# Attention, output projection and two-layer feed-forward on one core: three weight sums move from the head pairs to the output projection, and the last pair's products are interleaved anew

## The reference

```python
# 1: cross attention, 16 heads of 64; causal, so only the first 512 context rows count
qp = q @ Wq.T
k, v = jnp.split(latent_kv @ Wkv_expand.T, 2, axis=-1)
scores = jnp.where(causal, einsum(qh, kh) / 8, min)
out = softmax(scores) @ vh
x = x + out @ Wout.T
# 2: gated feed-forward whose weights are rounded to -1, 0, 1
scale = 1.0 / jnp.clip(jnp.mean(jnp.abs(w)), 1e-5, None)      # one number per weight matrix
wq = jnp.clip(jnp.round(w * scale), -1, 1) / scale
# rows are normalised and rounded to 8 bits; gate and up: 1024 x 2816 each; down: 2816 x 1024
# 3: a routed mixture of eight experts and a shared one
```

## Time and profile before

| | |
|---|---|
| median of 3 runs | 628.83 us (627.27 to 629.43) |
| profiled execution, its own time | 628.41 us |
| its span | 626.6 us |
| busy, share of the span | PE 97%, DVE 81%, ACT 68%, POOL 31% |
| first head pair's maxima to last pair's, 34.5 to 145.8 us | 111 us |
| output projection with the last pair's products, 145.8 to 200.2 us | 54 us |

### The profile page before, as it was taken

How to read it: one execution, slowest core, us unless ns; L and a number is a source line. 1 busy time by engine, 2 the same in 40 slices (tenths; PEclk the granted TensorE clock), 3 DMA queues, 4 the chain that set the end, 5 groups by cost and what they waited for, 6 DMA issues and landing times.

```text
span 626.6 us, 10596 instructions
## 1 busy us (share of the span) xinstructions
PE 609.7 (97%) x3611; PEld 477.3 (76%) x3625; DVE 507.1 (81%) x882; ACT 427.7 (68%) x563; POOL 193.3 (31%) x174
## 2 busy tenths in 40 slices
PE   7999999998999999999999999999999999999996
PEld 6778888887887444444567888898998989889775
DVE  5888888888787787889899479788696887968787
ACT  4998888889755988888585366649375583846630
POOL 2254445435000233435940310041340403304051
PEclk9999999999999999999999999999999999999999
DMA  8978776865246997936999758696775958769357
GB/s 332 411 304 305 304 306 243 310 268 201 101 141 242 416 366 278 386 129 249 405 357 422 318 199 331 243 355 243 301 301 212 390 216 312 290 235 373 115 176 269
DMA packets 31070, 177.91 MB, mean 284 GB/s; under 512 B 4064, under 2 KB 4064, under 8 KB 14784
## 3 DMA queue, kind: packets, MB, share of 16 engines
q1 hardware_dynamic: 25536, 158.64, 65.9%
q0 software_dynamic: 5504, 18.88, 8.3%
HBM read 154.30 MB, written 23.20 MB: 283 GB/s over the span
## 4 chain that ended last, share of the span: by engine, by line
PE 71%; ACT 13%; DVE 7%; issue 3%; DMA 3%; POOL 2%; DVEq 0%; POOLq 0%; SPq 0%; ACTq 0%
PE BK L2191 11%; PE BK L307 9%; PE BK L1892 8%; PE BK L1935 6%; PE BK L2194 4%; ACT RA L1384 4%; ACT PR L1411 4%; PE BK L313 3%; PE BK L314 3%; PE BK L319 3%; PE BK L2161 3%; PE BK L2149 2%; PE BK L1837 2%; DVE WL L1038 2%; PE BK L2147 2%
## 5 line engine op out<-in xcount | busy, mean ns | idle before, releaser
L2191 PE MATMUL BK<-EX,WH 128*128 128x320 f32 x384 | 99.4, 342 | 0.0
L705 POOL TENSOR_TENSOR WL<-RC,WH 128x2048 fp32r<-128x2048 f32 x7 | 45.5, 6506 | 167.7 <-ACT WH L1592 167.7
L1038 DVE TENSOR_TENSOR WL<-RA,WH 128x2048 fp32r<-128x2048 f32 x40 | 89.3, 2287 | 9.2 <-ACT WH L1592 8.8
L2194 PE MATMUL BK<-EX,WL 128*128 128x160 f32 x336 | 79.2, 236 | 0.0
L1592 ACT ACTIVATE WH<-RA 128x2048 fp32r<-128x2048 f32 x40 | 73.7, 1907 | 0.8 <-PE BK L1935 0.7
L2191 PEld LDWEIGHTS BK<-EX,WH 128*128 128x128 f32 x384 | 69.2, 189 | 0.0
L2194 PEld LDWEIGHTS BK<-EX,WL 128*128 128x128 f32 x336 | 64.1, 191 | 0.0
L655 POOL TENSOR_TENSOR HB<-HB,ND (+2 forms) x26 | 28.7, 1120 | 100.5 <-DVE BH L922 99.9
L1483 ACT ACTIVATE RA<-RA,RT 128x2048 int16<-128x2048 f32 x22 | 43.8, 1999 | 4.1 <-DMA RA<-wbit 2.1
L1701 ACT ACTIVATE HX<-SR 128x320 fp32r<-128x320 f32 x16 | 7.6, 472 | 57.0 <-DVE SR L1088 57.0
L1892 PE MATMUL BK<-TG,XQ 128*128 128x512 bf16 x189 | 42.1, 379 | 0.2
(11 more groups left out here) (335 smaller groups left out, 1666.2 us busy)
## 6 DMA issues: line engine op xcount, KB each, us to landing
RA<-wbit SPq DMA_DIRECT2D x54, 1024.0 KB, 6.8
RA<-wmoe SPq DMA_DIRECT2D x40, 1024.0 KB, 6.6
RC<-wmoe SPq DMA_DIRECT2D x20, 1024.0 KB, 7.9
rows<-ZERO POOLq DMA_DIRECT2D x40, 256.0 KB, 8.3
XG<-rows SPq DMA_DIRECT2D x10, 512.0 KB, 3.6
rows<-YS SPq DMA_DIRECT2D x9, 512.0 KB, 4.1
RA<-wqk SPq DMA_DIRECT2D x7, 640.0 KB, 8.6
RA<-wo SPq DMA_DIRECT2D x4, 1024.0 KB, 7.3
```

Of the source, the lines that this page charges most:

```text
L705: e.tensor_tensor(WL[2][:, at], RC[5][:, :], WH[2][:, at].bitcast(f32), ALU.subtract).then_inc(free_c[5], 1)
L1038: e.tensor_tensor(WL[m][:, q * RAW:q * RAW + RAW], RC[j][:, :], WH[m][:, q * RAW:q * RAW + RAW].bitcast(f32), ALU.subtract)\
L2191: mm = e.matmul(bank[GBK[f]][:, 0:2 * R], WH[m][:, at], EX[:, k, :, :].rearrange("p a b -> p (a b)"), start=k == 0, stop=k == KD - 1)
L2194: e.matmul(bank[GBK[f]][:, 0:R], WL[m][:, at], EX[:, k, 0, :], start=False, stop=False)
```

## The change

Three sums leave the head pairs: chunks 31 and 32 in pairs 3 and 4 (ACT, RA[4]) and chunk 30 in pair 7 (ACT, RA[1]). They are done by ACT after the last pair instead: chunk 30 and chunk 32 through a new buffer `RP`, which lies where the probabilities PR were, chunk 31 through RA[0]. `RP` is one buffer: SP loads chunk 32 into it when ACT has summed chunk 30. `WO_ORDER` becomes 3, 0, 1, 2: ACT writes the high part of block 3 where the sum of chunk 30 stood in pair 7, no longer between the exponentials and `probs_hi`. POOL makes the remainder of block 3 ahead of that of block 1. On PE, k = 6 of tile 0 comes ahead of the last pair's transposes, the matmuls of k = 2, 3 are split by which part of Wout they need, and the transposes are split by head. DVE adds the sums up inside `gate_rows(0)`, and PE's small matmul moves from behind tile 0 into tile 1.

```diff
-WO_IN = (6, 8, 9, 8)
+WO_IN = (4, 8, 9, 8)
-WO_ORDER = (0, 1, 3, 2)
+WO_ORDER = (3, 0, 1, 2)
+        RP = nc.alloc_sbuf_tensor_at("RP", [P, RAW], f32, offset=PR[0].manual_sbuf_range[0])
@@ SP
-            for c in (2, 3, 4):
-                pair_loads(c)
-                sum_load(4, (11, 31, 32)[c - 2], c)
-            with e.Fori(5, NPAIR - 1) as c:
+            pair_loads(2)
+            sum_load(4, 11, 2)
+            with e.Fori(3, NPAIR - 1) as c:
...
+            sum_load(2, 1, None)
+            e.wait_ge(s("wo_p"), 2)
             sum_load(3, 2, None)
-            e.wait_ge(s("wo_p"), 2)
-            sum_load(2, 1, None)
+            e.wait_ge(s("t_pe"), 2 * NPAIR)
+            e.dma_start(RP[:, :], wbit[30]).then_inc(in_x[0], 16)
+            e.wait_ge(s("wo_d"), 2)
+            sum_load(0, 31, None)
             e.wait_ge(s("ot_lo"), NPAIR + 1)
             e.dma_start(NG[:, :], n_gate.partition_broadcast(P)).then_inc(s("norm_in"), 16)
+            e.wait_ge(sum_x[0], 2)
+            e.dma_start(RP[:, :], wbit[32]).then_inc(in_x[0], 16)
@@ POOL
+            e.wait_ge(s("q_pe"), NPAIR)
+            wo_lo(3)
             wo_lo(1)
             e.wait_ge(s("pn"), 4 * NPAIR)
             v_lo(NPAIR - 1)
-            wo_lo(3)
@@ DVE
+            def weight_totals():
+
+                for j in range(2):
+                    e.wait_ge(sum_x[j], (3, 1)[j])
...
+                if t == 0:
+                    weight_totals()
                 o(e.tensor_reduce(col(6)[:, one], zt[:, :], AX.X, ALU.max, apply_absolute_value=True))
+                if t == 0:
+                    weight_scales()
@@ ACT
-                    absum(1, slice(30, 31), 16 * NPAIR)
+                    wo_hi(3)
                 q_split(c)
...
             exponentials(NPAIR - 1)
-            wo_hi(3)
             probs_hi(NPAIR - 1)
             e.wait_ge(s("vp_lo"), NPAIR)
             wo_hi(2)
-            absum_kept(4, 3, 16 * 7, None)
-            absum_kept(3, 2, 16 * (NPAIR + 1), (free_a[4], 6))
             out_hi(NPAIR - 1)
-            absum_kept(2, 1, 16 * (NPAIR + 1), (free_a[3], NPAIR))
+            absum_kept(4, 3, 16 * 5, None)
+            absum_kept(2, 1, 16 * (NPAIR + 1), (free_a[4], 4))
+            absum_kept(3, 2, 16 * (NPAIR + 1), (free_a[2], NPAIR))
+
+            def absum_late(chunk, n):
+                e.wait_ge(in_x[0], 16 * n)
+                e.activation(RP[:, :], RP[:, :], ACT.Abs, accum_out=ACCW[:, chunk:chunk + 1]).then_inc(sum_x[0], 1)
+            absum_late(30, 2)
+            absum(0, slice(31, 32), 16 * (WO_IN[2] + 1))
+            absum_late(32, 3)
@@ PE
+            def wout_part(ks, low):
+                for k in ks:
+                    for O, W in (((OTH, WOL),) if low else ((OTH, WOH), (OTL, WOH))):
+                        e.matmul(bank[YB[0][0]], O[:, k, 0:P], W[k // 2][:, k % 2, 0:512], start=False, stop=False)
             wout(0, 0, (0, 1), True, False)
             e.wait_ge(s("wo_p"), 1)
-            wout(0, 0, (2, 3), False, False)
-            transposes(NPAIR - 1)
+            e.wait_ge(s("ot_lo"), NPAIR)
+            wout(0, 0, (6,), False, False)
+            e.wait_ge(s("wo_hi"), WO_ORDER.index(1) + 1)
+            wout_part((2, 3), False)
+            transposes(NPAIR - 1, (0,))
+            e.wait_ge(s("wo_p"), 2)
+            wout_part((2, 3), True)
+            transposes(NPAIR - 1, (1,))
             attend(NPAIR - 1, False)
-            wout(0, 1, range(4), True, False)
+            wout(0, 1, (0, 1, 2, 3, 6), True, False)
...
-            e.wait_ge(s("wsum"), 1)
-            e.matmul(bank[7][:, 0:2], ONEF[:, :], WS[:, :], start=True, stop=True).then_inc(s("wsum_pe"), 1)
             for t in range(1, NT):
                 wout(t, 0, range(KD), True, True)
                 if t == 3:
                     e.wait_ge(s("wscale"), 1)
-                wout(t, 1, range(KD), True, True).then_inc(s("y_tile"), 1)
+                if t == 1:
+                    wout(t, 1, range(2), True, False)
+                    e.wait_ge(s("wsum"), 1)
+                    e.matmul(bank[7][:, 0:2], ONEF[:, :], WS[:, :], start=True, stop=True).then_inc(s("wsum_pe"), 1)
+                    wout(t, 1, range(2, KD), False, True).then_inc(s("y_tile"), 1)
+                else:
+                    wout(t, 1, range(KD), True, True).then_inc(s("y_tile"), 1)
                 rows_t(t - 1)
```

More of the change, by code:

```diff
@@ L450, in pair_loads @@
                     sum_load(j, c * 3 + 8 + j, c)
-            for c in (2, 3, 4):
-                pair_loads(c)
-                sum_load(4, (11, 31, 32)[c - 2], c)
-            with e.Fori(5, NPAIR - 1) as c:
+            pair_loads(2)
+            sum_load(4, 11, 2)
+            with e.Fori(3, NPAIR - 1) as c:
                 pair_loads(c)
             qk_load(NPAIR - 1)
-            e.wait_ge(free_a[4], 5)
+            e.wait_ge(free_a[4], 3)
             wo_load(0)
-            sum_load(1, 30, NPAIR - 1)
+            e.wait_ge(free_a[2], NPAIR - 1)
+            wo_load(3)
             e.wait_ge(free_a[3], NPAIR - 1)
             wo_load(1)
-            e.wait_ge(free_a[2], NPAIR - 1)
-            wo_load(3)
             e.wait_ge(free_a[0], NPAIR + 1)
             wo_load(2)
-            sum_load(1, 0, NPAIR)
+            sum_load(1, 0, NPAIR - 1)
             e.wait_ge(s("wo_d"), 1)
@@ L844, in _ @@
             out_lo(NPAIR - 1)
-            absum(1, slice(0, 1), 16 * (NPAIR + 1))
+            absum(1, slice(0, 1), 16 * NPAIR)
+            def weight_totals():
+                for j in range(2):
+                    e.wait_ge(sum_x[j], (3, 1)[j])
+                for j, n in ((0, NPAIR + 2), (1, NPAIR), (2, NPAIR), (3, NPAIR), (4, 4)):
+                    e.wait_ge(free_a[j], n)
+                e.tensor_reduce(WS[:, 0:1], ACCW[:, 0:2 * GC], AX.X, ALU.add)
+                e.tensor_reduce(WS[:, 1:2], ACCW[:, 2 * GC:NABS], AX.X, ALU.add).then_inc(s("wsum"), 1)
             def weight_scales():
@@ L881, in gate_scale @@
                     .then_inc(s("gscale"), 1)
[L882 to L886, removed]
-            e.tensor_reduce(WS[:, 1:2], ACCW[:, 2 * GC:NABS], AX.X, ALU.add).then_inc(s("wsum"), 1)
-            e.wait_ge(s("norm_in"), 32)
-            weight_scales()
             gate_rows(0)
@@ L1451, in pair @@
                     if isinstance(c, int):
-                        absum(4, slice(*((10, 11), (11, 12), (31, 32), (32, 33))[c - 1]), c * 16 + 16)
+                        absum(4, slice(9 + c, 10 + c), c * 16 + 16)
                     absum(3, bass.ds(c * 3 + 11, 1), c * 16 + 16)
@@ L1458, in pair @@
                 values_hi(c)
-            for c in (1, 2, 3, 4):
+            for c in (1, 2):
                 pair(c, True)
-            with e.Fori(5, NPAIR - 1) as c:
+            with e.Fori(3, NPAIR - 1) as c:
                 pair(c, True)
@@ L1487, in rounded_down @@
                 raw = down_raw(i)
-                arrived, n = {0: (in_x[0], 2), 1: (s("raw_d"), 1), 2: (in_x[1], 3), 3: (s("raw_e"), 1),
+                arrived, n = {0: (in_x[0], 4), 1: (s("raw_d"), 1), 2: (in_x[1], 3), 3: (s("raw_e"), 1),
                               4: (in_b[0], 6), 5: (in_b[1], 6), 6: (in_b[2], 5), 7: (in_b[3], 5),
@@ L1498, in down_sign @@
                     .then_inc(s("tern_a"), 1)
+            root(e, col(2)[:, 0:1], col(3)[:, 0:1])
             e.wait_ge(s("wscale"), 1)
@@ L1505, in sign @@
                     .then_inc(s("tern_a"), 1)
-            rounded(0, 0)
-            root(e, col(2)[:, 0:1], col(3)[:, 0:1])
-            for j in range(1, 4):
+            for j in range(4):
                 rounded(j, 0)
@@ L1811, in scores, with transposes @@
                         m.then_inc(s("s_pe"), 1)
-            def transposes(c):
-                for h in range(2):
+            def transposes(c, heads=(0, 1)):
+                for h in heads:
                     for n, (i, off) in enumerate(HBLK):
```

5 lines of the change are left out of this document (2 added, 3 removed).

## The result

The change takes 631.60 us in the median of 7 runs (630.04 to 632.30), the kernel before 628.66 us on the same chip (7 runs, 627.27 to 629.43). The ratio is 1.0040, 95% interval 1.0030 to 1.0049: slower, by 2.9 us in the medians. That is clear of the noise, though small. Profiled executions, which the sum of the prediction was made against: 630.04 us after (span 628.3), 628.41 before (span 626.6), +1.6 us.

The account below looks back on a forecast made before the run. PE, busy 97% of the span, was taken to bound the kernel. Terms -0.8 + 2.0 - 0.7 + 2.0 + 0.1 = +2.6 us gave 631.0 from the profiled execution, 631.4 from the median; stated 631.2 us, range 628.6 to 633.3.

Parts of the forecast that it names:

- Two sums out of pairs 3 and 4, -0.8: Head pairs 3 to 6: without ACT's fourth sum they take 62.33 us in place of 63.15, -0.8 us.
- The port block, 2.15 of the range 0 to 2.4: Last pair: DVE's block 0 subtraction waits for all of POOL's block 3 remainder, ending 2.15 us later.
- `attend` +2.0: Last pair: `attend`, released by the late `v_lo`, starts at 155.86 in place of 153.85, +2.0 us.
- k = 6 in the wait, -0.7: Ahead of `attend`: three k = 6 matmuls, formerly behind it, run in PE's wait, -0.7 us.
- The stall, 2.0: Middle of tile 1: PE's small matmul waits for chunk 32's load and sum, 2.0 us.
- E: The end of `attend`, from which the prediction counts the late sums, so that the earlier shift drops out.
- The rest, 0.1: Behind the stall: PE's transposes may wait for DVE's rounding of tile 0, 0.1 us at most.
- The one on the other side, no block: At 142.8: GpSimd does not block VectorE, the stall stays; +0.9 us, 629.6, chance 0.16.
- the one without a stall: Tile 1: sums finish before E + 14.35, so the small matmul doesn't wait; +0.5 us, 629.2, chance 0.12.
- Neither: Last pair and tile 1: no blocking and no stall; -1.2 us, 627.4, chance 0.07.

Follow-up runs that it names:

- Putting them back: Changed kernel with chunks 31 and 32 summed in pairs 3 and 4 again, only chunk 30 late: 630.14 us, ratio 1.0028 to the kernel before.
- memset: Changed kernel with GpSimd filling block 3's remainder with zeros in place of the subtraction: 628.28 us, ratio 0.9996 to the kernel before.
- VectorE first: Changed kernel with chunk 32 in its own buffer and GpSimd starting block 3's remainder only after VectorE's of block 0: 632.52 us, ratio 1.0056.
- second buffer: Changed kernel with chunk 32 loaded into a buffer of its own once the last `attend` is done: 628.84 us, ratio 1.0008 to the kernel before.
- block 1 first: Changed kernel with chunk 32's own buffer, GpSimd's order block 1, `v_lo`, block 3, and new PE, load and sum orders: 627.40 us, ratio 0.9983.
- the first kernel with the sums alone: Kernel before with the three sums moved, one buffer RP, its own product and remainder order, kept chunk 1 loaded late: 638.19 us, ratio 1.0156.
- the second chip: The unaltered change measured once more on another chip against the kernel before: 631.74 us, ratio 1.0045.
- the kernel with chunk 32 later still: Changed kernel with SP loading chunk 32 only after ACT has summed chunk 31: 634.18 us, ratio 1.0091 to the kernel before.
- the experiment with both edits: Changed kernel with block 3's remainder left out as zeros and chunk 32 in its own buffer: 626.64 us, ratio 0.9971 to the kernel before.

## Why the prediction was right

It said 631.2 us, slower, with a range of 628.6 to 633.3; it took 631.60. By its steps:

- **Two sums out of pairs 3 and 4, -0.8.** Measured 0.82 at pair 6. Putting them back cost 1.05 at the last maxima, so the size is 0.8 to 1.05.
- **The port block, 2.15 of the range 0 to 2.4.** DVE's subtraction ended at 146.57, and POOL's, begun at 139.80, would end at 144.43 by its own 4.63 us: 2.14 us apart, as in the one row of before that the number came from. DVE wanted to start a tenth of a microsecond earlier than I had reckoned, so the instruction was longer by 2.30, and the maxima were late by 2.11. The experiment with the memset took the block away and gave back 2.30 at `attend`. The rule of the Trainium skill that the prediction quoted ("SBUF — State Buffer", section "Who interferes with whom": the later of the two blocks fully) agrees with the 4.59 us here: by it DVE would end at 144.43 + 2.29 = 146.72, 0.15 us later than it did. The 6.03 us of the division in the kernel with VectorE first are not a case of that rule as quoted, since the division reads one large tile in SBUF and not two.
- **`attend` +2.0.** 154.90 for 153.85, and 0.82 from the pairs on top: 1.87. `v_lo` was its releaser, as said.
- **k = 6 in the wait, -0.7.** PE reached the small matmul at 173.40, that is 14.39 us after the end of `attend` (159.01); the prediction had 14.35, with these matmuls taken out.
- **The stall, 2.0.** It was 1.41. The mechanism is right and one term too large. The sum of chunk 30 was over at E + 8.49 (predicted 8.5), the load took 4.87 (4.9), and the last sum started at E + 13.40 (13.4). But from there to PE's matmul it took 2.40 us, not 2.96: the row that I took it from the earlier trace rows ends when PE got there, and PE was still busy with its matmuls. It was an upper bound and not a duration. With 2.40 in its place the same sum gives 1.45.
- **The rest, 0.1.** 0.33 us: `attend` 0.07 longer, and the small matmul 0.26 dearer behind a stall. I had not priced the latter.

The steps give -0.82 + 1.87 - 0.69 + 1.41 + 0.33 = +2.1 us, and the end is at +2.13; the prediction's steps had +2.6. Of the +2.13, 0.5 us are made good later, I have not traced where; the profiled execution is +1.6.

**What stays open.** The medians differ by 2.9 and 3.3 us on two chips, the two profiled executions of the change lie 1.6 us above that of before. That the median of 631.6 lies so near to the 631.2 is thus partly luck: the sum was 0.5 us too high for the trace, and something that the trace doesn't show adds 1.2 to 1.7. The four kernels with one or both of the costs removed also came out 0.5 to 1.0 us below my expectations, which were added up from the waits in the trace and the change's median. In the kernel with the stall alone (memset) and in those with the block alone (second buffer, two sums back) the median lies within 0.4 us of the profiled execution; with both it lies 1.6 and 1.7 us above. Some kernels without both costs show part of such a distance: 0.6 us with block 1 first, 0.9 with VectorE first, and 1.3 in the first kernel with the sums alone. A clock that falls in some executions would do that, since it fell behind the longer stalls. But in both profiles of the change it is 1.00, and the mean clock that was read with every execution speaks against it: the slowest ones of the change (631.77 to 632.30, and 633.15 on the second chip) have 0.999, a faster one (630.15) 0.998, while the kernel with chunk 32 later still, where a fall cost 1.6 us, has 0.996 and 0.997. The cause of this part stays open.

**The rivals.** The one on the other side, no block, was refuted by the 4.59 us, the one without a stall by the wait of 1.4. *Neither* is what the experiment with both edits makes: 1.7 us faster than before, where I had 1.2 in the prediction.

## What to carry to other kernels

Where VectorE and GpSimd both subtract tiles in SBUF, count the second one's start from the end of the first, and place the overlap where nobody waits: every order that I tried had one (4.59, 6.03, 3.97, 2.81, 3.66 us). Between VectorE first and block 1 first lie 5.1 us at the end of the projection (204.25 and 199.15); a part of them is the clock's fall, and the two differ in their loads, sums and first matmuls too. When work is moved out of a stretch bound by one engine, ask for its last transfer and for what stands in line behind it: one buffer used twice cost 1.7 us at the end of the projection, and the same loads and sums in another order cost 7.2 us. A hand-over read off a row in which the receiver was still busy is a bound, not a duration.

## What the runs showed of the hardware that I had not expected

A stall of PE costs more than its length once it is long enough for the granted clock to fall. With stalls of 1.2 to 1.4 us the clock stayed at 1.00 in the profiles, and the next 18 matmuls took 4.21 us. After 3.41 us it was 0.82 and 0.84 in the next two stretches of 5 us, and they took 5.82 us; after 5.33 us 0.51 and 0.81, and 6.18 us; after 7.69 us 0.69 and 0.63, and 5.87 us. In stretches of half a microsecond the value is 1.00, the upper level (2.4 GHz), or 0.50, the lower (1.2 GHz), but for the ones in which it changes. After the 3.41 us it fell only at about 178.2, when PE had been at work again for over 1 us (from 176.79); after the two longer stalls it was at 0.50 already when PE went on. On these 18 matmuls the clock cost 1.6 to 2.0 us in each of the three kernels, without growing with the stall. The kernel with VectorE first shows the same with two smaller gaps 5.4 us apart (1.70 us until 149.12 and 3.04 us until 154.48): 0.94 and 0.72 in the two stretches of 5 us from 150 to 160 us.

Also, DVE's division is four instructions. In the kernel with VectorE first, one of the four was over before POOL's second subtraction had well begun (149.1), the next spans it, and 0.69 us of the 1.27 lie behind its end (153.74): a short series is no protection against a long instruction of the other engine.
